# Own score banks for the first batch's maxima, two banks for the convolution's products, another order of the first loads, and no meeting of the engines before the experts

## What is computed

```python
# 1. dynamic mixing over 31 neighbours in 4 heads, then a convolution of 31 taps
logits = (x @ Wl.T + bl).reshape(Bq, Tq, H, K);  w = softmax(where(valid, logits, -inf))
y = einsum('bthk,btkhd->bthd', w, xg) + bias
z = selu(conv(y, Wc, 'VALID') + bc)          # 128 -> 512 channels, 720 tokens left
h = z @ W2.T + b2
# 2. causal attention of width 64; a stage that adds the layer norm back
h = h + attn(layernorm(h))
h = h + layernorm(h)      # what is left of a stage whose own outputs lie past channel 127
# 3. attention of 720 queries over 7200 keys and values per batch, layer norm inside
h = h + cross_attn(layernorm(h), k, v)
# 4. two shared experts and 64 routed ones, top 6, capacity 540
h = h + experts(layernorm(h))
```

## Time and profile before

| | us |
|---|---|
| median of 3 runs | 1616.63 (1615.47 to 1623.19) |
| the profiled execution, its own time | 1626.76 |
| its span | 1625.0 |
| PE busy | 1517.1 |
| DVE, ACT, POOL busy | 1060.9, 722.8, 577.3 |

### The profile page before, as it was taken

How to read it: one execution, slowest core, us unless ns; L and a number is a source line. 1 busy time by engine, 2 the same in 40 slices (tenths; PEclk the granted TensorE clock), 3 DMA queues, 4 the chain that set the end, 5 groups by cost and what they waited for, 6 DMA issues and landing times. The chain is left out here.

```text
span 1625.0 us, 30403 instructions
## 1 busy us (share of the span) xinstructions
PE 1517.1 (93%) x11596; PEld 1014.1 (62%) x11596; DVE 1060.9 (65%) x2085; ACT 722.8 (44%) x1272; POOL 577.3 (36%) x632
## 2 busy tenths in 40 slices
PE   2899998898899889999999999999998999999998
PEld 2556765655566567777777777778884444444444
DVE  4765545555555667777868786865456876876766
ACT  2231122111211145556655555556665655465554
POOL 2120001000110267713360236000994654556555
PEclk6899999999999999999999999999999999999999
DMA  8330100110000167932251134000223443344443
GB/s 212 97 112 23 29 26 17 30 33 27 21 14 19 30 132 170 178 64 61 60 118 40 47 79 118 15 24 1 66 84 98 128 128 99 120 133 133 138 130 106
DMA packets 143775, 128.44 MB, mean 79 GB/s; under 512 B 86838, under 2 KB 124174, under 8 KB 142606
## 3 DMA queue, kind: packets, MB, share of 16 engines
q1 hardware_dynamic: 127053, 110.62, 26.3%
q0 software_dynamic: 2272, 12.06, 2.5%
q10 hardware_dynamic: 14304, 3.81, 1.2%
HBM read 106.21 MB, written 5.28 MB: 69 GB/s over the span
## 5 line engine op out<-in xcount | busy, mean ns | idle before, releaser
L973 ACT ACTIVATE region_c<-ps 128x720 f16<-128x720 f32 (+1 forms) x228 | 175.6, 770 | 252.8 <-PE ps L1864 252.7
L845 POOL TENSOR_TENSOR region_k<-region_c,region_k 128x480 f16<-128x480 f32 x198 | 217.6, 1102 | 174.5 <-ACT region_k L1095 174.5
L1339 DVE TENSOR_TENSOR region_c<-ps,region_c 128x720 f16<-128x720 f32 (+1 forms) x228 | 205.9, 903 | 93.9 <-ACT ps L974 91.4
L1698 PE MATMUL ps<-region_k 128*128 128x360 f16 (+1 forms) x752 | 242.8, 323 | 5.2 <-ACT m L952 5.2
L1700 PE MATMUL ps<-region_k 128*128 128x360 f16 (+1 forms) x752 | 242.0, 322 | 0.0
L1699 PE MATMUL ps<-region_k 128*128 128x360 f16 (+1 forms) x752 | 241.9, 322 | 0.0
L1344 DVE TENSOR_REDUCE region_c<-ps 120x1 f32<-120x512 f32 x252 | 173.4, 688 | 85.8 <-PE ps L1829 83.7
L728 POOL TENSOR_TENSOR vare<-mv,eps 120x6 f32<-120x6 f32 x20 | 4.0, 198 | 497.3 <-DVE mv L1246 497.3
L1890 PE MATMUL ps<-region_k,region_c 128*120 128x129 f16 (+1 forms) x1368 | 180.2, 221 | 0.0
L1891 PE MATMUL ps<-region_k,region_c 128*120 128x128 f16 (+1 forms) x1368 | 179.3, 220 | 0.0
L974 ACT ACTIVATE ps<-ps 128x720 f32<-128x720 f32 (+1 forms) x228 | 174.4, 765 | 0.0
(11 more groups left out here) (277 smaller groups left out, 2822.7 us busy)
## 6 DMA issues: line engine op xcount, KB each, us to landing
gates<-gates_dram SPq DMA_DIRECT2D x384, 120.0 KB, 2.8
region_c<-in_k SPq DMA_DIRECT2D x56, 256.0 KB, 2.9
region_c<-in_v SPq DMA_DIRECT2D x56, 256.0 KB, 3.1
region_c<-in_WcT POOLq DMA_DIRECT2D x8, 1024.0 KB, 6.5
region_c<-in_experts SPq DMA_DIRECT2D x18, 352.0 KB, 3.0
gates<-band_dram SPq DMA_DIRECT2D x26, 189.0 KB
region_c<-in_k POOLq DMA_DIRECT2D x14, 256.0 KB, 3.0
region_k<-region_c SPq DMA_TRANSPOSE x120, 3.1
```

Of the source, the lines that this page charges most:

```text
L845: g.tensor_tensor(a_lo[u], ac[u], a_hi[u], ALU.subtract).then_inc(s["a_lo_ready"], 1)
L973: a.activation(halves(p_hi[u][0:parts]), st, ACT.Exp).then_inc(s["p_hi_ready"], 1)
L1339: v.tensor_tensor(halves(p_lo[u][0:parts]), two(2 * u, parts), halves(p_hi[u][0:parts]), ALU.subtract).then_inc(s["lo_ready"], 1)
L1698: mm(o, wh[:, m, j], xh[:, j:j + w], start=(j == 0), stop=False)
```

## The change

Six edits, in the diff below (lines that do not matter here are left out):

1. Maxima: a bank of their own. `max_slot` gives a maximum bank 2, and from quarter 6 of batch 3 on every odd one bank 3. PE now waits for the reader of the last maximum in the same bank (`first_free`). There are 28 maxima in batch 2 (before 40) and 57 in batch 3 (before 45), some quarters of which have two. The shift is made after the last product of the stage instead of one quarter earlier.
2. The products alternate between banks 0 and 1 (`product_bank`), so that PE waits for the reader of the product before the last.
3. `sums` of the first two pieces of weights move behind the split in `MIX_ALONE`.
4. Loads: `xw` of the first six bands first, the constants only behind the last band of batch 0; the first piece of convolution weights and the zero fill of the bands no longer wait.
5. The products of weight matrices (`weight_products`) move from the start into the convolution of batch 0.
6. `stage_end` is gone; PE waits for the weights of the experts (`wf_done`) and for the readers of banks that it takes over.

```diff
 MIX_ALONE = ([("logits", 0), ("taps", 0), ("logits", 1), ("taps", 1), ("high", 0), ("low", 0), ("high", 1),
-              ("low", 1), ("sums", 0), ("sums", 1), ("band", 0)]
+              ("low", 1), ("band", 0)]
              + [x for j in range(NW - 1) for x in (("band", j + 1), ("apply", j))]
-             + [("apply", NW - 1), ("split", 0)])
+             + [("apply", NW - 1), ("split", 0), ("sums", 0), ("sums", 1)])
...
-    if b not in (B - 2, B - 1):
+    first = [at for at in range(QUARTERS) if at % 12 in (1, 2, 3, 5, 6, 9, 10)]
+    if b == B - 2:
+        return list(zip(first, range(len(first))))
+    if b != B - 1:
         return []
-    spread = [at for at in range(QUARTERS) if at % 12 not in (0, 8)]
-    if b == B - 2:
-        return list(zip(spread, range(len(spread))))
-    return [(at, len(spread) + at) for at in range(R * NCH + 1 - len(spread))]
+    times = sorted(list(range(QUARTERS - 2)) + [at for at in range(QUARTERS - 2) if at % 12 in (2, 6, 10)])
+    return list(zip(times, range(len(first), R * NCH + 1)))
+
+def max_slot(n):
+    last = dict((k, at) for at, k in max_steps(B - 1))
+    return 3 if last.get(n, 0) >= 6 and (n % 2 or n == R * NCH) else 2
+
+def slot_before(n):
+    return max([k for k in range(n) if max_slot(k) == max_slot(n)], default=None)
...
-        steps.append((QUARTERS - 2, (MAX, 0, "shift", 0)))
+        steps.append((QUARTERS - 1, (MAX, 0, "shift", 0)))
...
-def stage_end(eng, n):
-            eng.drain()
-            eng.sem_inc(s["stage"], 1)
-            eng.wait_ge(s["stage"], 5 * n)
+def product_bank(b, m, p):
+            return (MC * b + m + p) % 2
...
# SP
-            for dst, name in const_loads:
-                sp.dma_start(dst[:], d[name]).then_inc(s["const_in"], 16)
-            for n, name in enumerate(row_loads):
-                sp.dma_start(rows[:, n, :], d[name].partition_broadcast(P)).then_inc(s["const_in"], 16)
+            for j in range(NBAND):
+                u, _ = band_buffer(0, j)
+                sp.dma_start(xw[u], d["xw"][j]).then_inc(s_band[u], 16)
...
# POOL
-            pool.wait_ge(s["zero_out"], 32)
             for n in range(2):
+                if n:
+                    pool.wait_ge(s["zero_out"], 32)
                 pool.dma_start(wc_f[n], d["WcT"][n]).then_inc(s_wc[n], 16)
...
# ACT, ahead of the zero fill of band_dram
-            act.wait_ge(s["mix_in"], MIX_IN)
...
# DVE
             def first_maximum(n):
-                turn, bk = shared(0, "max", n, MAX)
-                dve.wait_ge(s["shared_full"], turn)
+                dve.wait_ge(s["first_ps"], n + 1)
...
-                    for *_, n in early:
+                    for n in early[:1]:
                         first_maximum(n)
                     if quarter == 3:
                         product_done(b, m, p)
+                    for n in early[1:]:
+                        first_maximum(n)
...
# PE
-                _, bk, left, _ = SHARED[MAX, 0, "max", n]
-                pe.wait_ge(s[left[0]], left[1])
+                slot, left = max_slot(n), slot_before(n)
+                if left is not None:
+                    pe.wait_ge(s["first_free"], left + 1)
+                elif slot == 3:
+                    pe.wait_ge(s["dve_read"], SHARED[DOWN, B - 2, "h", 1][3])
...
-                    if turn >= 3:
-                        pe.wait_ge(s["prod_free"], turn - 2)
+                    if turn >= 2:
+                        pe.wait_ge(s["prod_free"], turn - 1)
...
-            pe.wait_ge(s["wprod_sb"], 1)
...
+                    if (b, m, p, quarter) == (0, 1, 0, 0):
+                        weight_products()
...
+            pe.wait_ge(s["wf_done"], 3 * NWP)
             for n in range(SETS):
+                if n == SETS - 1:
+                    pe.wait_ge(s["post_free"], len(USE) - len(beside(B, "pe")))
                 up(n)
```

More of the change, by code:

```diff
@@ L132, in layer_order @@
     for i in range(QUARTERS):
-        yield (i // 12, i // 4 % 3, i % 4, [x for at, x in steps if at == i - 0.5],
-               [x for at, x in steps if at == i])
+        yield i // 12, i // 4 % 3, i % 4, [n for at, n in max_steps(b) if at == i], [x for at, x in steps if at == i]
 def shared_turns():
@@ L144, in shared_turns @@
             kind, at, what, k = x
-            if what not in ("logits", "band", "apply", "h", "max"):
+            if what not in ("logits", "band", "apply", "h"):
                 continue
@@ L492, in tower @@
             gate_ps up_ps up_free silu_done a_ready a_hi_ready a_lo_ready down_done
-            out_cm_ready out_ps fin_ready fin_out
-            stage""".split()
+            out_cm_ready out_ps fin_ready fin_out""".split()
         s = {n: sem(n) for n in names}
@@ L756, in _ @@
                 work = [(at + 0.25, "power", 3 * (b - 1) + x[3] + 1) for at, x in side_steps(b) if x[2] == "stats"]
-                work += [(at - 0.25, "keys", n // R + 1) for at, n in max_steps(b) if n % R == 0 and 0 < n < R * NCH]
+                work += [(at + 0.1, "keys", n // R + 1) for at, n in max_steps(b) if n % R == 0 and 0 < n < R * NCH]
                 for _, what, n in sorted(work):
@@ L948, in _, with weight_products @@
                 mix(0, what, k)
[L950 to L953, removed]
+            def weight_products():
+                act.wait_ge(s["wprod_ps"], 1)
+                for n, (dst, scale) in enumerate(((g0, 64 ** -0.5), (m0, 1.0), (g1, C ** -0.5), (m1, 1.0))):
+                    last = a.activation(dst[:], bank(6)[:, 128 * n:128 * (n + 1)], ACT.Copy, scale=scale)
+                last.then_inc(s["wprod_sb"], 1)
             for b in range(B):
                 for m, p, quarter, early, steps in layer_order(b):
+                    if (b, m, p, quarter) == (0, 1, 0, 0):
+                        weight_products()
                     if quarter == 3:
@@ L1218, in product_done @@
                 else:
-                    own.link(v.scalar_tensor_tensor(out=z_odd, in0=bank(2)[:, 0:HALF], scalar=1 / W_SCALE,
+                    own.link(v.scalar_tensor_tensor(out=z_odd, in0=bank(bk)[:, 0:HALF], scalar=1 / W_SCALE,
                                                     in1=z_odd, op0=ALU.mult, op1=ALU.add))
@@ L1666, in first_maximum @@
                 pe.wait_ge(s["k16_ready"], n // R + 1)
[L1667 to L1675 removed]
+                slot, left = max_slot(n), slot_before(n)
[3 more added lines that the diff above has]
+                    pe.wait_ge(s["dve_read"], SHARED[DOWN, B - 2, "h", 1][3])
+                q, keys = q_hi[:, 0, n % R * P:(n % R + 1) * P], k16[n // R % 2]
+                if n == R * NCH:
+                    for r in range(R):
+                        last = mm(bank(3, P)[:, r * TAIL:(r + 1) * TAIL], q_hi[:, 0, r * P:(r + 1) * P],
+                                  keys[:, 0:TAIL], start=True, stop=True)
+                else:
+                    last = mm(bank(slot, P), q, keys, start=True, stop=True)
+                last.then_inc(s["first_ps"], 1)
             def conv(b, m, p, quarter, early):
@@ L1690, in conv @@
                 w = HALF + (p == 0)
-                o = bank(p)[:, 0:w]
+                o = bank(product_bank(b, m, p))[:, 0:w]
                 xh, xl = ys[b % 2][p]
@@ L1695, in conv @@
                     if j % 4 == 2:
[L1696 removed]
+                        for row in early[:1]:
                             first_maximum(row)
@@ L1702, in conv @@
                     last.then_inc(s["prod_full"], 1)
+                for row in early[1:]:
+                    first_maximum(row)
             pe.wait_ge(s["mix_in"], MIX_IN)
@@ L1718, in _ @@
                     conv(b, m, p, quarter, early)
+                    if (b, m, p, quarter) == (0, 1, 0, 0):
+                        weight_products()
+                    if b == 0 and (m, p, quarter) == (MC - 1, 2, 3):
+                        pe.wait_ge(s["wprod_sb"], 1)
                     for kind, at, what, k in steps:
```

69 lines of the change are left out of this document (34 added, 35 removed).

## The result

The changed kernel takes 1597.56 us (median of four runs, 1596.40 to 1599.23), beside 1616.05 us before (four runs, 1613.48 to 1623.19): ratio 0.9862, 95% interval 0.9842 to 0.9883. That is 19 to 26 us less, where 29.8 us were predicted. A second group of runs gave 1595.36 beside 1619.85 us (ratio 0.9846, 0.9826 to 0.9867). The profiled execution took 1597.52 us in its own time, 1595.7 of them span, at a mean clock of 0.978.

What follows compares the result with a forecast made beforehand. PE was taken to bound the convolution, with holes, and weight-piece loading the start. Terms -9.5 - 20 - 2.5 + 4.4 - 2.2 = -29.8 us took 1616.63 to 1587 us, range 1575 to 1603.

Steps and rivals of the forecast that it cites:

- The start, -9.5 us: Before the convolution: four edits let it begin at 44 to 46 us instead of 54.30, 9.5 us won.
- If the write takes some 3 us less, the bands are read from about 21: Start, band reads: a faster write lets the first read, issued at 23.80 us before, come at about 21.
- the second rival: Start: shared transfer engines keep band reads as late as before; only 3.2 us won, 1593 us in all; chance 0.17.
- the `sums` come again free of cost: Start: sums moved behind the split save 2.2 us and return as two DVE instructions before the third product.
- Waits of bank 3, -20 us: Late convolution: of 26.5 us of PE waits for bank 3, 6.5 stay and 20 are won.
- The stay of 2.6 us forecast for 407 us: Convolution at 407.43 us: PE passes the maximum but stops at the band needing the same bank; some 2.6 us stay.
- Clock in that stretch, -2.5 us: Late convolution: with fewer waits the clock falls at fewer places, 2.5 us won.
- Two product banks, nothing: Convolution: alternating two banks for products costs nothing, with some 7 us of cover per product.
- No product's first matmul waits: Convolution: a sign that no product's first matmul waits for a product's reader.
- The shift, +4.4 us: Between convolution and `DOWN`: the shift behind the last selu delays what follows by 3.6 us, plus 0.8 for the clock.
- The meeting, -2.2 us: Between attention and experts: PE and ACT go on without waiting for all engines, 2.2 us won.

Runs made afterwards that it cites:

- Giving the inputs their time back: Changed kernel, but zero fill, first weight piece and xw loads wait until the logits' inputs have landed: 1597.14 us, ratio 0.9858 to the kernel before.
- The start alone: Kernel before with only the edits to sums, weight products, load order, and zero fill and first piece without waits: 1618.65 us, ratio 0.9992.
- the second profile of before: Kernel before, unaltered, run and profiled once more: 1615.58 us in one run.
- the earlier shift: Changed kernel with the shift made one quarter earlier, beside the convolution's last product: 1586.33 us, ratio 0.9786 to the kernel before.
- holding the pieces back: Changed kernel, shift one quarter earlier, third and fourth weight pieces held until the seventh apply: 1586.72 us; second piece also delayed, first piece and xw behind inputs: 1589.29 us.

## Why the prediction was right, and where it was not

The time lies in the range, the sign was right, and the point was 10 us too low.

- **The start, -9.5 us: wrong in size and in kind.** By the profile -3.8 at the convolution's beginning, by timing -1.3 (3.4 less to 0.8 more). Two steps failed. First, "If the write takes some 3 us less, the bands are read from about 21". The write did take less (5.7 us instead of 9.4), but the step left its issue at 14.38 us, and it moved to 18.93: the first piece, zero fill and xw came beside the logits' inputs (landed at 10.54 us instead of 5.69), and DVE's last step of the taps took 1.98 us beside POOL's sum. Giving the inputs their time back won nothing, since the zero fill then landed at 18.5. This was the second rival, with 3.2 us. Second, that the `sums` come again free of cost and that the convolution's beginning sets the end. They stand in front of batch 1's logits, whose chain to the first band ends at 86 us in either kernel. Moving the beginning by another 3.6 us, or back by 3.5, changed nothing measurable. That 8 us more at the start would have been lost there as well is only argued from this.
- **Waits of bank 3, -20 us: right.** The start alone gives 1.3 us by timing, product banks and meeting nothing that timing can tell, and the shift loses time. So by elimination the banks of the maxima carry the change; no run put the maxima back into the shared bank. PE's idle time from 240 us to the end of the convolution went from 35.5 to 16.1 us, 19.4 less. The stay of 2.6 us forecast for 407 us is there with 2.5, the others are 5.4 beside a forecast of 3.9. The part that one private bank gives is the larger one; the second bank is worth 4.4 us of waits, 3 to 6 us by timing.
- **Clock in that stretch, -2.5 us: size not settled.** Busy time fell by 10.6 us against the first profile of before and by 4.0 against the second.
- **Two product banks, nothing: right by timing.** "No product's first matmul waits" was wrong by one wait of 1.18 us.
- **The shift, +4.4 us: right in mechanism, 1 us too small.** The stretch from the convolution to `DOWN` went from 4.4 to 9.3 us (7.5 to 8.5 forecast), 4.9 more where 3.6 were forecast. The shift's own seven instructions take 3.7 us, as forecast. The term that was put at nothing is the matmuls of `key_scores` between shift and `DOWN`: they take 1.54 us (551.16 to 552.70), and before they ran while PE waited for the selu in any case. The 0.8 us for the clock came out as 0.3 to 0.6 (4.85 us for `DOWN`'s first 24 matmuls beside 4.55 and 4.30). Up to the 128x32 matmuls behind `DOWN` 5.4 us are lost in all, against the second profile. The 9.0 us that the earlier shift gives are not this loss alone: 1.8 us are gained beyond the kernel before, and 1.7 lie in the experts.
- **The meeting, -2.2 us: -2.0 by the profiles** (8.40 to 6.43 us). Timing could not tell it from nothing.

The stages of the second profile of before and of the changed kernel, in us, each from the end of the one above:

| | before | changed | difference |
|---|---|---|---|
| up to the convolution | 54.7 | 50.5 | -4.2 |
| convolution, to its last matmul | 512.1 | 492.9 | -19.2 |
| from there through `DOWN`, to the 128x32 matmuls behind it | 13.2 | 18.6 | +5.4 |
| attention, to its last matmuls | 633.1 | 635.1 | +2.0 |
| meeting and experts | 400.8 | 398.7 | -2.1 |
| span | 1613.8 | 1595.7 | -18.1 |

The second row holds the 19.4 us of idle time and 4.0 of clock, less the 4.2 us of the first row, which are lost again in it. The 2.0 us of attention, where no edit is, are clock. The medians differ by 18.5 and 24.5 us. So the forecast was some 5 to 11 us too much, and its term for the start was too large by 8. That the first profile of before and that of the changed kernel differ by 29.2 us, just the forecast, is chance: the one of before was longer than the second by 11.2 us, 6.6 of them in the convolution by its clock.

The kernel with the early shift, 1586.33 us, beats both kernels; holding the pieces back adds nothing to it.

## What to carry to other kernels

An earlier beginning of a stage is worth what the next meeting with a chain of its own leaves of it: find that meeting (here batch 1's first band at 86 us) before counting the gain, and look whether the work that was moved now stands in front of that chain. A side step of 3.4 us that is moved behind the last product costs more than its own time: the matmuls that wait for it come behind it, and what follows may run at the lower clock. Here that was 7.2 us up to attention, against the same step one quarter earlier. And profile the kernel before twice: two executions of it differed by 11 us, half of the effect, with the same waits.

## What the hardware showed

**DVE held up by POOL.** DVE's addition of 96x124 elements from two buffers in SBUF takes 0.28 us alone and 2.82 at 59.28 us, ending at 62.10, while POOL's addition ran from 59.58 for 2.37 us, to 61.95. It ended just after POOL's. Its record starts 0.30 us ahead of POOL's, so the rows do not show which of the two asked first. This agrees with the Trainium skill, "SBUF — State Buffer", section "SBUF: two separate sides", by which an operation of DVE with two inputs in SBUF and one of GpSimd that reads SBUF take turns at a shared pair of ports, each for a whole instruction.

**Dips of the clock move about.** From `DOWN` to the end of attention, with the same program there, the changed kernel took 644.3 us and the kernel with one bank for maxima 639.0. One window of the changed kernel, then the same of that one (same columns as above):

```profile
819.60:826.40 6.80, 6.80 (x34) 4.92 (x34) 1.30 (x2) 1.43 (x2) 5.81 (x7) 0.50 0.77 192
```

```profile
819.60:826.40 6.80, 6.80 (x69) 5.30 (x68) 4.79 (x7) 3.93 (x7) 4.08 (x6) 1.00 0.83 204
```

In the first, PE was busy for the whole 6.80 us at 1.2 GHz and did 34 matmuls, in the second 69. Some 5 us come or go in this way with no edit in the stage. What decides at which of the small waits the clock falls was not found. It hides effects of that size in single profiles.
